# A fused decoder layer with routed experts: small constant additions, sign changes and score scaling move to ScalarE, running counts join the ranks on TensorE

## What is computed

```
x = x + self_attention(layernorm(x))              # 16 heads of 8, rotary positions, causal softmax
x = x + cross_attention(layernorm(x), ctx, ctx)   # scores without softmax; inside: residual + layer norm, gain, bias
x = x + ffn(layernorm(x))                         # 8 experts, top-1
```

```
aff    = x @ centroids.T            # 8 affinities of a token
assign = argmax(aff, axis=1)
h      = relu(layernorm(x)*g_e + b_e) @ w1_e ...  # 512 hidden features
y      = x + h @ w2_e + b2_e
alpha  = sigmoid(aff of the chosen expert)
out    = alpha*y + (1 - alpha)*x
```

## Time and profile before

| | us |
|---|---|
| median of 3 runs | 602.0 |
| lowest, highest run | 600.85, 604.33 |
| the profiled execution, its own time | 606.41 |
| its span, first to last instruction | 604.2 |

### The profile page before, as it was taken

How to read it: one execution, slowest core, us unless ns; L and a number is a source line. 1 busy time by engine, 2 the same in 40 slices (tenths; PEclk the granted TensorE clock), 3 DMA queues, 4 the chain that set the end, 5 groups by cost and what they waited for, 6 DMA issues and landing times.

```text
span 604.2 us, 26574 instructions
## 1 busy us (share of the span) xinstructions
PE 543.7 (90%) x8719; PEld 430.0 (71%) x8719; DVE 485.4 (80%) x1762; ACT 463.6 (77%) x1304; POOL 434.1 (72%) x852
## 2 busy tenths in 40 slices
PE   4789999999999999999999999978887988999995
PEld 2467767766766666676676666756786977999894
DVE  3787999888998989998899998987676666777673
ACT  2777777877888878888778787775776775899893
POOL 3334788888988989888998888877665566354553
PEclk9799999999999999999999999999899999999999
DMA  6421111322112312122111121102112122322210
GB/s 174 56 77 30 29 38 39 96 68 58 54 56 78 88 56 56 55 84 81 55 38 40 51 62 38 30 20 71 28 47 60 52 65 70 83 72 67 60 54 14
DMA packets 55189, 35.46 MB, mean 59 GB/s; under 512 B 14976, under 2 KB 50433, under 8 KB 55056
## 3 DMA queue, kind: packets, MB, share of 16 engines
q1 hardware_dynamic: 50160, 24.44, 15.5%
q0 software_dynamic: 4320, 8.66, 4.3%
q10 hardware_dynamic: 576, 0.66, 0.4%
HBM read 24.46 MB, written 9.74 MB: 57 GB/s over the span
## 4 chain that ended last, share of the span: by engine, by line
PE 84%; issue 6%; ACT 3%; DVE 3%; SPq 1%; another core or an unknown queue 1%; DVEq 1%; DMA 0%; POOLq 0%; POOL 0%; ACTq 0%
PE side L963 9%; PE side L764 8%; PE quad L701 6%; PE side L668 5%; PE quad L733 5%; PE side L948 5%; PE quad L948 5%; PE side L825 5%; PE side L678 3%; PE side L861 3%; PE side L879 3%; PE side L833 2%; PE side L795 2%; PE quad L747 2%; PE side L846 2%
## 5 line engine op out<-in xcount | busy, mean ns | idle before, releaser
L2046 POOL DMA_INDIRECT out<-yo,rb x71 | 69.9, 984 | 74.9 <-DVE yo L1784 45.6
L963 PE MATMUL side<-w,hT 128*128 x568 | 79.5, 284 | 8.7 <-DVE hT L1574 6.8
L1073 ACT ACTIVATE ex<-qk,cf 128x512 f32<-128x512 f32 x128 | 85.4, 718 | 0.0
L1432 DVE TENSOR_REDUCE mx<-quad 128x16 f32<-128x1024 f32 x64 | 75.3, 1218 | 10.9 <-PE quad L701 10.8
L963 PEld LDWEIGHTS side<-w,hT 128*128 128x128 f32 x568 | 71.5, 197 | 11.6 <-issue 11.0
L2013 POOL DMA_INDIRECT expert_rows<-pay,sli x64 | 68.6, 1072 | 12.8 <-issue 12.8
L1092 ACT ACTIVATE prob<-quad 128x1024 f32<-128x1024 f32 x64 | 62.1, 1022 | 18.6 <-PE quad L747 18.6
L764 PE MATMUL side<-prob,vau 128*32 128x64 f32 x2048 | 50.9, 223 | 14.5 <-issue 12.6
L764 PEld LDWEIGHTS side<-prob,vau 128*32 128x32 f32 x2048 | 36.7, 109 | 24.9 <-issue 17.0
L1564 DVE TENSOR_SCALAR xh<-rb 128x128 f32<-128x128 f32 x71 | 25.1, 354 | 27.8 <-issue 24.4
L1189 ACT COPY w1b<-w 128x512 f32 x71 | 43.7, 617 | 0.0
(11 more groups left out here) (276 smaller groups left out, 1610.2 us busy)
## 6 DMA issues: line engine op xcount, KB each, us to landing
rb<-expert_rows SPq DMA_DIRECT2D x71, 68.0 KB
xin<-in_x SPq DMA_DIRECT2D x32, 128.0 KB
cin<-in_ctx SPq DMA_DIRECT2D x32, 128.0 KB
xr<-in_x SPq DMA_DIRECT2D x32, 128.0 KB, 2.3
w<-in_w1t SPq DMA_DIRECT2D x8, 256.0 KB
w<-in_w2t SPq DMA_DIRECT2D x8, 256.0 KB
out<-yo,rb POOLq DMA_INDIRECT x71
expert_rows<-pay,sli POOLq DMA_INDIRECT x64
```

Of the source, the lines that this page charges most:

```text
L963: last = mm(YB[u][:, 0:D], hT[u][:, c, :], w2[:, bass.ds(e, 1), c, :], start=c == 0, stop=c == FC - 1)
L1073: act(ex[g.par][:, i, :, :].rearrange("p a t -> p (a t)"), qk[g.par][:, :, :].rearrange("p a t -> p (a t)"), ACT.Copy, scale=own4[:, i:i + ...
L1432: v.tensor_reduce(mx[g.par][:, 2 * h_:2 * h_ + 2, :], quad[:, 2 * h_:2 * h_ + 2, :].rearrange("p r (h k) -> p r h k", k=SQ), AX.X, ALU.max ...
L2046: v.indirect_dma_start(out=o_rows, out_offset=bass.IndirectOffsetOnAxis(ap=number, axis=0), in_=yo[b.c % 4][:, :], in_offset=None, bounds_ ...
```

## The change

On ScalarE there are new steps: `var_x`, `var_x1`, `var_x2` and a third instruction in `squares` add the constant 1e-5 (and change the sign of the mean), with a stage `ac_v` of their own; `scaled_scores` comes from VectorE, there one instruction over both tiles and three score groups with a factor of 1.0 for the third, now four instructions in place that leave the third out. The GpSimd steps keep only the powers and products, and wait for ScalarE instead. On TensorE a matrix product of the identity with the running counts opens the accumulation of `ranks`, so VectorE's `place` goes and `counted` becomes a copy; `slots` and `slot_numbers` are joined.

```diff
-        po_l = stage_steps("pool_norm_x", "eps pow")
+        ac_v = stage_steps("act_variances", "eL | eT nT | eU | eR eR2")
+        po_l = stage_steps("pool_norm_x", "pow")
...
@@ TensorE, ranks
                 free(g, "ranks")
                 bank_ = at("ranks", g)
+                wait(pe, dv_r, g.n - 1, "tot")
+                mm(bank_[:, 0:(J + 1) * E].rearrange("p (a e) -> p a e", e=E), identf,
+                   cnt[:, :].unsqueeze(1).broadcast_to((P, J + 1, E)), start=True, stop=False)
                 mm(bank_[:, 0:(J + 1) * E], tri_b[:, :], ohb[g.par][:, :, :].rearrange("p j e -> p (j e)"),
-                   start=True, stop=False)
+                   start=False, stop=False)
...
@@ ScalarE
             def squares(g):
...
+                wait(ac, po_t, g.n - 2, "pow2")
+                wait(ac, ac_t, g.n, "s1")
+                act(ve["U"][g.par][:, :], ss[g.par][:, :], ACT.Copy, scale=1.0 / D, bias=EPS
+                    ).then_inc(*ac_v.done("eU"))
+
+            def var_x(g):
+                wait(ac, po_l, g.n - 2, "pow")
+                wait(ac, dv_l, g.n, "a1")
+                act(ve["L"][g.par][:, :], mv["L"][g.par][:, :, 1], ACT.Copy, bias=EPS).then_inc(*ac_v.done("eL"))
+
+            def var_x1(g):
+                wait(ac, po_t, g.n - 2, "std")
+                wait(ac, po_t, g.n - 2, "mr")
+                wait(ac, dv_t, g.n, "a1")
+                act(ve["T"][g.par][:, :], mv["T"][g.par][:, :, 1], ACT.Copy, bias=EPS).then_inc(*ac_v.done("eT"))
+                act(ng[g.par][:, :], mv["T"][g.par][:, :, 0], ACT.Copy, scale=-1.0).then_inc(*ac_v.done("nT"))
+
+            def var_x2(g):
+                wait(ac, po_r, g.n - 2, "pow")
+                wait(ac, dv_r, g.n, "a1")
+                act(ve2[g.par][:, :, 0], pay[g.par][:, :, C_V], ACT.Copy, bias=EPS).then_inc(*ac_v.done("eR"))
+                act(ve2[g.par][:, :, 1], pay[g.par][:, :, C_V], ACT.Copy, scale=1.0 + EPS, bias=EPS * EPS
+                    ).then_inc(*ac_v.done("eR2"))
+
+            def scaled_scores(g):
+                wait(ac, dv_t, g.n, "y1")
+                wait(ac, po_t, g.n, "pow2")
+                for j in range(J):
+                    for a in range(2):
+                        own = slice(D + a * E, D + (a + 1) * E)
+                        last = act(y1[g.par][:, j, own], y1[g.par][:, j, own], ACT.Copy,
+                                   scale=sc[g.par][:, j, a:a + 1])
+                last.then_inc(*ac_r.done("ab"))
...
             def one(g):
                 stage(g, 5, attended)
                 stage(g, 3, exp, 0)
                 stage(g, 3, exp, 1)
+                stage(g, 6, scaled_scores)
+                stage(g, 0, var_x)
                 stage(g, 0, norm_x)
+                stage(g, 4, var_x1)
                 stage(g, 4, norm_x1)
                 stage(g, 5, squares)
                 stage(g, 1, values)
                 stage(g, 0, x_turned)
                 stage(g, 5, token_ids)
+                stage(g, 6, var_x2)
                 stage(g, 4, x1_turned)
...
@@ VectorE
             def affinities(g):
-                wait(dv, dv_r, g.n, "ab")
+                wait(dv, ac_r, g.n, "ab")
...
             def counted(g):
-                wait(dv, dv_r, g.n, "rk")
-                v.tensor_tensor(cnt[:, :], cnt[:, :], at("ranks", g)[:, J * E:(J + 1) * E], ALU.add
-                                ).then_inc(*dv_r.done("tot"))
+                wait(dv, pe_r, g.n, "rank")
+                v.tensor_copy(cnt[:, :], at("ranks", g)[:, J * E:(J + 1) * E]).then_inc(*dv_r.done("tot"))
...
-                stage(g, 8, place)
                 stage(g, 8, own_rank)
...
-                stage(g, 7, scaled_scores)
...
@@ GpSimd
             def std_x(g):
                 wait(po, ac_l, g.n - 2, "n")
-                wait(po, dv_l, g.n, "a1")
-                v.tensor_scalar(u[:, :], mv["L"][g.par][:, :, 1], EPS, None, ALU.add).then_inc(*po_l.done("eps"))
-                wait(po, po_l, g.n, "eps")
+                wait(po, ac_v, g.n, "eL")
...
             def std_x1(g):
...
+                wait(po, ac_v, g.n, "eT")
                 v.tensor_tensor(r_[:, :], ...half..., ALU.pow).then_inc(*po_t.done("pow"))
                 wait(po, po_t, g.n, "pow")
+                wait(po, ac_v, g.n, "nT")
...
             def std_x2(g):
-                wait(po, dv_r, g.n, "a1")
-                v.tensor_scalar(ve2[g.par][:, :, 0], px[:, :, C_V], EPS, None, ALU.add).then_inc(*po_r.done("eps"))
-                v.tensor_scalar(ve2[g.par][:, :, 1], px[:, :, C_V], 1.0 + EPS, EPS * EPS, ALU.mult, ALU.add
-                                ).then_inc(*po_r.done("eps2"))
-                wait(po, po_r, g.n, "eps2")
+                wait(po, ac_v, g.n, "eR2")
...
```

More of the change, by code:

```diff
@@ L268, in decoder_kernel @@
         pay = two("pay", [P, J, ROW])
-        sc = two("sc", [P, J, 3])
-        tm = two("tm", [P, J, 3, E])
+        sc = two("sc", [P, J, 2])
         af = two("af", [P, J, E])
@@ L1138, in squares @@
             def squares(g):
-                wait(ac, po_t, g.n - 2, "eps2")
                 wait(ac, dv_t, g.n, "y1")
@@ L1248, in step @@
                 return e2
+            scaled_scores(g28)
             attended(g29)
@@ L1252, in _ @@
             exp(g31, 1)
+            var_x2(g28)
             e0, e1 = first_two(Block(0))
+            var_x1(g30)
             norm_x1(g30)
@@ L1265, in _ @@
                     attended(g30)
+                if c == 4:
+                    var_x2(g29)
                 if c == 5:
@@ L1274, in _ @@
                     x1_turned(g31)
+                if c == 12:
+                    var_x2(g30)
                 if c == 13:
                     cross_queries(g31)
-                if c == 14:
+                if c == 15:
                     exp_affinity(g30)
-                if c == 15:
                     attended(g31)
@@ L1283, in _ @@
                     token_ids(g31)
-                if c == 24:
+                if c == 20:
+                    scaled_scores(g31)
+                if c == 23:
+                    var_x2(g31)
+                if c == 25:
                     exp_affinity(g31)
@@ L1394, in stats_x @@
             def stats_x(g):
-                wait(dv, po_l, g.n - 2, "eps")
+                wait(dv, ac_v, g.n - 2, "eL")
                 wait_dma(dv, d_x, g)
@@ L1488, in y_sum @@
                 first(dv, g, s_vec, 1)
-                wait(dv, dv_r, g.n - 2, "ab")
+                wait(dv, dv_r, g.n - 2, "af")
                 wait(dv, ac_t, g.n, "n")
@@ L1587, in alpha, with counted @@
                 v.reciprocal(pay[g.par][:, :, C_AL], ea1[g.par][:, :]).then_inc(*dv_r.done("al"))
-            def place(g):
-                wait(dv, dv_r, g.n - 1, "tot")
-                wait(dv, dv_r, g.n - 2, "sl")
+            def counted(g):
                 wait(dv, pe_r, g.n, "rank")
-                v.tensor_tensor(rk[g.par][:, :, :], at("ranks", g)[:, 0:J * E].rearrange("p (j e) -> p j e", e=E),
-                                cnt[:, :].unsqueeze(1).broadcast_to((P, J, E)), ALU.add
-                                ).then_inc(*dv_r.done("rk"))
-            def counted(g):
-                wait(dv, dv_r, g.n, "rk")
-                v.tensor_tensor(cnt[:, :], cnt[:, :], at("ranks", g)[:, J * E:(J + 1) * E], ALU.add
-                                ).then_inc(*dv_r.done("tot"))
+                v.tensor_copy(cnt[:, :], at("ranks", g)[:, J * E:(J + 1) * E]).then_inc(*dv_r.done("tot"))
                 if g.n == GT - 1:
@@ L1609, in own_rank @@
             def own_rank(g):
[L1611 to L1614 removed]
+                wait(dv, dv_r, g.n - 2, "sl")
+                wait(dv, pe_r, g.n, "rank")
+                v.tensor_tensor(rk[g.par][:, :, :], at("ranks", g)[:, 0:J * E].rearrange("p (j e) -> p j e", e=E),
+                                ohb[g.par][:, 0:J, :], ALU.mult).then_inc(*dv_r.done("pr"))
             def slots(g):
@@ L1850, in leftovers @@
                 if c == 25:
-                    place(g31)
+                    own_rank(g31)
                     counted(g31)
-                    own_rank(g31)
                     wait(dv, dv_r, g31.n, "tot")
@@ L1870, in _ @@
             rows_in(Block(2))
-            place(g28)
+            own_rank(g28)
             counted(g28)
@@ L1959, in std_y @@
             def std_y(g):
-                u = ve["U"][g.par]
                 wait(po, dv_r, g.n - 2, "w1")
-                wait(po, dv_r, g.n - 2, "ab")
-                wait(po, ac_t, g.n, "s1")
-                v.tensor_scalar(u[:, :], ss[g.par][:, :], 1.0 / D, EPS, ALU.mult, ALU.add).then_inc(*po_t.done("eps2"))
+                wait(po, ac_r, g.n - 2, "ab")
+                wait(po, po_t, g.n, "pow")
                 v.tensor_tensor(sc[g.par][:, :, 1], ve["T"][g.par][:, :], rs["T"][g.par][:, :], ALU.mult
                                 ).then_inc(*po_t.done("std"))
-                wait(po, po_t, g.n, "eps2")
```

(6 more changed lines are left out.)

75 lines of the change are left out of this document (23 added, 52 removed).

## The result

The changed kernel takes **921.7 us** (median of 4 runs, 918.97 to 925.5); the kernel before takes 603.2 beside it (4 runs, 600.85 to 604.46). The ratio is **1.529, interval 1.521 to 1.538**. The forecast was 858 with a range of 770 to 905: the direction and the ring of waits came out, the size did not; the result lies 17 us above the range. The profiled execution took 923.9 us with a span of 921.0.

What follows compares the result with a forecast made beforehand. TensorE was taken to set the 12.51 us round. New waits make it 21.9 with clock losses: 26 x 9.4 = 244 us, plus 12 for the last two rounds, giving 862 profiled, 858 us median, range 770 to 905.

Steps and rivals of the forecast that it cites:

- the ring of waits: Chain through ScalarE, VectorE, TensorE and GpSimd closing on itself one round later: 20.2 us instead of 12.51, +7.7.
- Steps 1 to 6: One round's chain, from exponentials through scalings, `y_sum`, `values`, `xT` and `var_x2`, `max_low`, `max_rows` to next exponentials: 20.2 us.
- Step 3: TensorE's `values` waits for `y_sum` of four groups earlier, sharing a bank; starts at 6.97, `x_turned` ends at 10.02.
- The shorter loop: Ring inside ScalarE and GpSimd through constants, powers and norms: a round of 18.5 us, covered while the long chain holds.
- the clock term: TensorE's two idle spells per round bring half clock afterwards: 1.7 us for both, making a round of 21.9.
- 20 to 23 us named as a sign: Sign that the forecast is right: one round in the middle takes 20 to 23 us.
- The second part: Kernel's part after the rounds, near 180 us: steps dealt out ahead of users, so 0, bounds -3 and +6.
- Worse: Rival: both clock losses whole, 28 x 11.1 = 311, so 913 us; chance 0.10.
- the clock would not fall: Rival: the long chain without clock losses, or with them where they cost nothing: 813 us; chance 0.15.
- the short loop alone: Rival: bank wait on `y_sum` not binding, only the ScalarE and GpSimd loop left: 770 us; chance 0.09.
- Only busy time counts: Rival: ScalarE's added 1.4 us vanishes in its 2.3 us of idle time: 602 us, no change; chance 0.02.
- faster: Rival: GpSimd and VectorE had held TensorE back, so relieving them gains 9 us: 593 us; chance 0.02.

Runs made afterwards that it cites:

- the round at full clock with extra products: Changed kernel with 12 and 14 useless extra matrix products in TensorE's two idle stretches, groups 5 to 27: 851.4 us; this round 19.96 us.
- the kernel with `affinities` late: Changed kernel with VectorE's `affinities` and `largest` moved behind `y_sum`: 780.1 us (one run).
- the opened ring: Changed kernel with the same instructions, each new ScalarE step placed ahead of its user on GpSimd or VectorE: 606.8 us, ratio 1.0079.
- the kernel with the ranks alone: Kernel before with only the running counts added by TensorE's product and VectorE's `place` gone: 607.2 us, ratio 1.0068.

## Why the forecast was right, and where it failed

The steps of the forecast against both traces, in us after the start of the exponentials. The first column is the forecast without the clock; the second the changed kernel; the third the round at full clock with extra products:

| step | forecast | changed | full clock |
|---|---|---|---|
| 1: scalings end | 2.70 | 2.69 | 2.70 |
| 2: `y_sum` ends | 6.87 | 6.72 | 6.73 |
| 3: `values` starts | 6.97 | 7.42 | 6.99 |
| 4: `xT` starts | 10.12 | 11.77 | 10.15 |
| 4: `var_x2` done | 10.83 | 12.43 | 10.81 |
| 5: `max_low` ends | 17.24 | 18.61 | 17.01 |
| 6: `max_rows` starts | 17.34 | 19.43 | 17.39 |
| next exponentials | 20.2 | 23.93 | 19.96 |

**Steps 1 to 6 held in their times.** At full clock none is off by more than 0.24 us, the round included. Some of that closeness is errors that cancel: `values` starts 0.26 us behind `y_sum` and `max_rows` 0.38 behind `max_low`, where the forecast had 0.10 each, and against it `var_x2` to the end of `max_low` took 6.20 us (forecast 6.41) and `max_rows` to the exponentials 2.57 (2.87). Step 3 named the wrong wait: `values` followed `weighted`, which waited for `rotate`, and not `y_sum`. Since `rotate` and `y_sum` stand 0.5 us apart behind the same scalings on VectorE, the time hardly tells; a version without the bank wait on `y_sum` was not run. The price of four scalings, taken as the middle between two rows, came to 0.86 us in the trace (forecast 0.87). The shorter loop, forecast at 18.5 without clock losses, was 18.3 at a clock of 0.81 in the kernel with `affinities` late. That busy time would not decide held too: the opened ring has the same work and 12.55 us rounds.

**The failed step is the clock term**: "I take half: 1.7 us for both, bounds 0 and 3.4". It measured 3.97, above its own upper bound, and with it the round of 23.93 lies over the 20 to 23 us named as a sign. The bound came from the earlier trace rows, where one idle stretch was followed by 3.4 us at 0.50. Here two idle stretches (TensorE busy 0.00 for 2.5 us from 385.80 and for 3.4 from 399.20) each come with 6.8 us at half clock, twice that, so 13.6 of 23.93 us. The fall comes while TensorE is still idle:

```profile
387.90:388.30 0.40, 0.00 (x0) 0.00 (x0) 0.38 (x1) 0.25 (x1) 0.22 (x2) 0.50 0.00 0
...
401.70:402.60 0.90, 0.00 (x0) 0.00 (x0) 0.78 (x5) 0.90 (x3) 0.90 (x3) 0.50 0.00 0
```

TensorE starts again at 388.38 and 402.70, so only 0.6 and 1.3 us of the two spells are idle time, the part by which the forecast had argued for the half. The rest covers `values` to `x_turned` (3 of 4.35 us) and all from `attended` to the exponentials. By segments, the changed kernel against the full-clock round: +0.43 to the start of `values`, +1.19 to `xT`, +0.42 to `max_rows`, +1.93 to the exponentials. The last is the dearest: L715 to the exponentials takes 4.50 us, in the kernel before 2.87, and TensorE is busy for all of it. With 3.97 in place of 1.7 the sum gives 26 x 2.27 = 59 us more: 862 + 59 = 921 for the profiled execution, which took 923.9. That it comes so close is luck: the middle rounds come out 10 us too dear by it (24.2 in place of 23.97 after, 12.51 in place of a mean of 12.71 before), and the terms below 12 us too cheap.

The Trainium skill (TensorE: Matmul & The Clock Gate, HAM oscillation) describes such a kernel, there waiting for DMA, in which every wait sends TensorE back to the low clock, and reckons the loss as the cold time by 1 - 1.2/2.4. By that rule 13.6 us would cost 6.8 a round; the runs say 3.97, since part of the cold time is idle or beside the chain. So here the rule is an upper bound. The forecast's bound of 3.4 is the same sum on two spells of 3.4 us: what failed in it is the length of the spells, taken from one case.

**Smaller terms.** Rounds before 6 were costed at 0 and took 4.1 us: rounds 4 and 5 are 14.2 us long, since `var_x` is there already: GpSimd waits 5.68 us for it at 59.85. The last two rounds, forecast at 12, took 14.8. The second part, 0 within -3 and +6, took 4.3. VectorE was to lose 0.4 us a round and lost 0.1 (11.22 to 11.13 in the opened ring). The counts' product, 0.26, takes 0.30 and costs some 4 us where TensorE is the bound (the kernel with the ranks alone). Not in the forecast were the waits of `values_keys` on `x1_sum`, of `weighted` on `rotate` and of `attended` on `counted`. The full-clock round has all three. The last costs 0.3 us there; all three keep TensorE's own work back and so shape its idle stretches.

**The rivals.** "Worse" (both clock losses whole, 913 us, chance 0.10) is the nearest, and its place was right: the clock on the work of the chain. It was given too little, as each loss had been bounded by one spell of 3.4 us. That the clock would not fall (813) is excluded by 0.72 over the middle rounds, and the short loop alone (770) by the 205.2 us that `affinities` waited: with that wait moved off the chain, the time fell to 780. "Only busy time counts" and "faster" are excluded by the waits, and by the opened ring, which gave ScalarE its head start and reached 606.8: even then the 1.4 us that GpSimd was spared (11.26 to 9.85) bought nothing.

## What to carry to other kernels

Where engines work through lists in order, an instruction's price is where it stands: ask of each result that a change moves to another engine how far ahead of its user it is made, and follow the chain round until it meets itself. If it does within one round, the sum along it is the new round, however idle the engines are. And cost TensorE's idle time together with what it does to the clock afterwards: the half-clock spell was twice as long here as the one seen in the kernel before, which is seldom idle, and it fell on the work that the chain needs first.
